# A sum over scan states: from identity matmuls to accumulated transpositions, with the mixer's end placed one or two units later

## The reference

```
h = layernorm(x) * (1 + ca) + sa;  x = x + ga * causal_attention(h)        # 8 heads, latent keys and values
h = layernorm(x) * (1 + cb) + sb;  x = x + gb * experts(h)                 # 8 small experts, best 2
h = layernorm(x) * (1 + ca) + sa;  x = x + ga * mixer(h)                   # the state-space mixer, below
h = layernorm(x) * (1 + cb) + sb;  x = x + gb * experts(h)                 # 8 experts of 512, best 2

mixer(h):  x_in, res = split(h @ in_w + in_b)                              # 256 channels each
           xc = silu(causal_conv4(x_in));  d, Bm, Cm = split(xc @ x_proj_w + x_proj_b)
           delta = softplus(d @ dt_w + dt_b);  dA = exp(delta * A);  dBx = delta * xc * Bm
           state[n, t] = dA[n, t] * state[n, t-1] + dBx[n, t]              # 16 states n per channel
           y[t] = sum over n of state[n, t] * Cm[n, t]  + xc * D_skip
           return (y * silu(res)) @ out_w + out_b
```

## Time and profile before

| | us |
|---|---|
| median of 3 runs | 1374.36 (1373.46 to 1374.67) |
| span of the profiled execution | 1379.8 |
| PE busy in the span | 1207.2 (87%) |
| DVE busy | 1037.0 (75%) |
| ACT busy | 852.2 (62%) |
| POOL busy | 489.3 (35%) |
| mean granted clock of TensorE, share of full speed | 0.95 |

### The profile page before, as it was taken

The page is one execution under the profiler, slowest core; times in us unless marked ns, Lnnn a source line. Parts: engine busy times, 40 slices in busy tenths (PEclk is TensorE's granted clock), DMA queues, the critical chain, the costliest instruction groups (busy, mean ns, idle before and its releaser), DMA issues. The chain is left out here.

```text
span 1379.8 us, 19465 instructions
## 1 busy us (share of the span) xinstructions
PE 1207.2 (87%) x6560; PEld 760.5 (55%) x6560; DVE 1037.0 (75%) x2381; ACT 852.2 (62%) x1600; POOL 489.3 (35%) x309
## 2 busy tenths in 40 slices
PE   5974689989998889989999889989899899889698
PEld 3651145655665556555656456655656556555456
DVE  3666977599866997589866997579975998569822
ACT  2634446488646966489565866479664876469332
POOL 0103930078002950069100960049300870029300
PEclk8995579999999999999999999999999999999899
DMA  7101100030001200020001200021000300011000
GB/s 245 70 16 64 60 8 1 16 108 16 16 17 55 69 12 6 16 92 31 17 9 43 88 1 17 16 78 47 16 1 16 109 16 9 1 64 60 8 1 8
DMA packets 18514, 53.22 MB, mean 39 GB/s; under 512 B 4976, under 2 KB 5864, under 8 KB 18032
## 3 DMA queue, kind: packets, MB, share of 16 engines
q1 hardware_dynamic: 16112, 43.40, 9.8%
q0 software_dynamic: 1296, 4.20, 1.0%
q10 hardware_dynamic: 1008, 4.38, 0.8%
HBM read 45.40 MB, written 2.38 MB: 35 GB/s over the span
## 5 line engine op out<-in xcount | busy, mean ns | idle before, releaser
L1482 DVE TENSOR_TENSOR_SCAN probs_T<-bank,probs_T 128x512 f32<-128x512 f32 x256 | 303.9, 1212 | 16.1 <-ACT bank L1078 12.1
L618 PEld LDWEIGHTS bank<-w_w,hidden 128*128 128x128 f32 x2048 | 248.8, 192 | 72.9 <-issue 66.8
L602 PE MATMUL bank<-hT,w_w 128*128 128x512 f32 x512 | 262.9, 629 | 27.1 <-ACT hidden L933 26.2
L447 POOL TENSOR_TENSOR probs_T<-step_space,probs_T 128x1024 f32<-128x1024 f32 x120 | 282.2, 2358 | 5.9 <-DVE probs_T L1482 5.7
L618 PE MATMUL bank<-w_w,hidden 128*128 128x128 f32 x2048 | 251.6, 276 | 2.1 <-DVE expert_sum L1174 1.6
L933 ACT ACTIVATE hidden<-bank,w_b 128x512 f32<-128x512 f32 x256 | 169.6, 686 | 117.5 <-PE bank L602 116.9
L1006 ACT ACTIVATE probs<-bank,row_neg 128x128 f32<-128x128 f32 (+3 forms) x256 | 134.8, 528 | 151.7 <-DVE row_neg L1335 134.8
L1078 ACT ACTIVATE bank<-step_space,a_neg 128x512 f32<-128x512 f32 x256 | 167.8, 683 | 55.0 <-DVE probs_T L1482 36.7
L701 PE MATMUL bank<-k_pad,q_lat 128*128 128x512 f32 (+3 forms) x512 | 185.3, 448 | 5.8 <-DMA k_pad<-xc 5.8
L1335 DVE TENSOR_REDUCE row_neg<-bank 128x1 f32<-128x128 f32 (+3 forms) x256 | 123.5, 487 | 85.1 <-PE bank L703 82.7
L602 PEld LDWEIGHTS bank<-hT,w_w 128*128 128x128 f32 x512 | 89.0, 194 | 153.0 <-ACT hidden L933 97.0
(11 more groups left out here) (183 smaller groups left out, 1577.6 us busy)
## 6 DMA issues: line engine op xcount, KB each, us to landing
probs_T<-b_rows_dram SPq DMA_DIRECT2D x64, 512.0 KB, 3.7
w_w<-in_w_dram ACTq DMA_DIRECT2D x2, 2048.0 KB, 14.0
k_pad<-xc SPq DMA_DIRECT2D x64, 64.0 KB, 2.0
x_in<-in_x_dram POOLq DMA_DIRECT2D x8, 256.0 KB, 3.3
gate<-gate_rows_dram SPq DMA_DIRECT2D x1, 2048.0 KB, 7.0
out_dram<-x_out POOLq DMA_DIRECT2D x7, 256.0 KB, 2.8
step_space<-in_wmod_dram SPq DMA_DIRECT2D x1, 768.0 KB, 5.6
probs_T<-in_wqT_dram SPq DMA_DIRECT2D x1, 512.0 KB, 4.1
```

What stands on the lines that cost most here:

```text
L447: ins = nc.gpsimd.tensor_tensor(inject[:, n % 3, :, :], u[:], row.unsqueeze(1).to_broadcast([P, DH, T]), ALU.mult)
L602: mm(hid1_bank(n)[:], w["w1"][:, n // C1, n % C1 * P:(n % C1 + 1) * P], hT[3][:], start=True, stop=True).then_inc(hid1_mm.sem, 1)
L618: ins = mm(to[:, t * P:(t + 1) * P], hidden[:, (e * C1 + c) % (2 * C1), t * P:(t + 1) * P], w["w2"][:, e * C1 + c, :], start=(c == 0), sto ...
L1482: v.tensor_tensor_scan(state[:, n % 2, c, :], decay(DH * n + c)[:], inject[:, n % 3, c, :], 0.0, ALU.mult, ALU.add).then_inc(st_ok.sem, 1)
```

## The change

PE no longer multiplies the first half's product with the identity on the left. It takes each of the product's four 128x128 tiles as the stationary operand, with the identity as the moving one, and transposes it into bank 7, accumulating over the states (`sum_first`: four instructions for each state in place of one matmul). The bank then holds the transpose of the sum, tile by tile. At the end ACT copies the bank into SBUF (`take_sum`, new, into the space of `state_sum`), and PE transposes the four tiles back into bank 7 (`turn_sum`, new), from where `mixer_end` reads as before, waiting for `sum_T` in place of `sum_mm`.

In the attention `take_sum` stands on ACT at unit 3, after the unit's exponential, and `turn_sum` on PE at unit 5. The out projection goes from unit 6 to 7, the two parts of `mixer_end` from 3 and 7 to 5 and 8, `finish` from 5 to 4, the copy of x and the layernorm from 8 to 9, and each step of the experts' head one unit later: PE's to 17, 19, 26 and 29, ACT's to 18, 23 and 27, DVE's to 21, 24 and 33. In the tail `take_sum` and `turn_sum` follow the last sum directly.

```diff
--- before.py
+++ after.py
@@ -190,6 +190,7 @@
         split = sb("split", [3 * BC, T], BF16)
         dt_in, delta, u = (step_space[:, k, :, :] for k in range(3))
         state_sum, y_skip, z = dt_in, delta, u
+        sum_rows = state_sum[:, 0, :]
 
 
         bank = [ctx.enter_context(nc.psum_tensor(f"bank{i}", [P, T], F32)) for i in range(8)]
@@ -307,6 +308,8 @@
         rd_ok = signal("rd_ok", NS)
         acc_ok = signal("acc_ok", NS - 1)
         sum_mm = signal("sum_mm", NS)
+        sum_out = signal("sum_out", 1)
+        sum_T = signal("sum_T", 1)
         z_ok = signal("z_ok", DH)
         mix_mm = signal("mix_mm", 1)
         mix_add = signal("mix_add", 1)
@@ -660,13 +663,22 @@
 
             def sum_first(n):
 
-                mm(bank[SUM_BANK][:], ident[:], read[:, n % 2, 0, :], start=(n == 0), stop=(n == NS - 1)
-                   ).then_inc(sum_mm.sem, 1)
+                for t in range(NT):
+                    ins = mm(bank[SUM_BANK][:, t * P:(t + 1) * P], read[:, n % 2, 0, t * P:(t + 1) * P], ident[:],
+                             start=(n == 0 and t == 0), stop=(n == NS - 1), is_transpose=True, skip_group_check=True)
+                ins.then_inc(sum_mm.sem, 1)
 
             def last_sum(b):
 
                 pe.wait_ge(rd_ok.sem, rd_ok.at(b, NS))
                 sum_first(NS - 1)
+
+            def turn_sum(b):
+
+                pe.wait_ge(sum_out.sem, sum_out.at(b, 1))
+                for t in range(NT):
+                    ins = tr(bank[SUM_BANK][:, t * P:(t + 1) * P], sum_rows[:, t * P:(t + 1) * P], ident[:])
+                ins.then_inc(sum_T.sem, 1)
 
             def mixer_out_mm(b):
                 pe.wait_ge(z_ok.sem, z_ok.at(b, DH))
@@ -754,6 +766,8 @@
                         scores(n)
                     if n >= LAG:
                         transposes(n - LAG)
+                    if behind and n == TURN_SUM:
+                        turn_sum(b - 1)
                     if behind and n == PE_MIXER:
                         mixer_out_mm(b - 1)
                     if not behind and n in SETUP_PE:
@@ -890,6 +904,7 @@
             main(B - 1, True, False, True)
             scan(B - 1, True)
             last_sum(B - 1)
+            turn_sum(B - 1)
             pe.wait_ge(out1_add.sem, out1_add.at(B - 2, E * NT + 1))
             mixer_out_mm(B - 1)
 
@@ -943,6 +958,10 @@
                 act.wait_ge(gap_in.sem, gap_in.at(b, layer + 1))
                 f(gap_tanh[:], gap[:], ACT.Tanh, scale=0.5).then_inc(gap_out.sem, 1)
 
+            def take_sum(b):
+                act.wait_ge(sum_mm.sem, sum_mm.at(b, NS))
+                f(sum_rows[:], bank[SUM_BANK][:], ACT.Copy).then_inc(sum_out.sem, 1)
+
             def take_queries(b, g):
                 act.wait_ge(q_mm.sem, q_mm.at(b, g + 1))
                 f(q_lat[:, g, :], bank[PRE_BANK][:], ACT.Copy).then_inc(q_out.sem, 1)
@@ -1005,6 +1024,8 @@
                         act.wait_ge(p_T.sem, p_T.at(b, n - 3))
                     f(probs_ring[:, n % 4, 0:(i + 1) * P], bank[SCORE_BANK[n % 4]][:, 0:(i + 1) * P], ACT.Exp,
                       bias=row_neg[:, n % 4:n % 4 + 1], accum_out=row_sum[:, g, i, j:j + 1]).then_inc(s_exp.sem, 1)
+                    if behind and n == LAST_SUM:
+                        take_sum(b - 1)
                     if behind and n in ACT_HEAD:
                         expert_head(b - 1, ACT_HEAD.index(n))
                     if not behind and n == SETUP_ACT:
@@ -1100,6 +1121,7 @@
             for b in range(1, B - 1):
                 iteration(b, True, True)
             iteration(B - 1, True, False)
+            take_sum(B - 1)
             expert_head(B - 1, 0)
             for n in range(E * C1):
                 if n in (2, 4):
@@ -1293,7 +1315,7 @@
                 if k == 0:
                     for c in range(DH):
                         if c == 0:
-                            dve.wait_ge(sum_mm.sem, sum_mm.at(b, NS))
+                            dve.wait_ge(sum_T.sem, sum_T.at(b, 1))
                             total = bank[SUM_BANK][:]
                         else:
                             dve.wait_ge(acc_ok.sem, acc_ok.at(b, NS - 1))
@@ -1530,9 +1552,9 @@
 PRE_UNIT = 22
 ALL_BY_ACT = 12
 LAG = 3
-LAST_SUM, LAST_READ, PE_MIXER, DVE_MIXER, FINISH, TAKE_X, NORM_UNIT = 3, 2, 6, (3, 7), 5, 8, 8
-
-PE_HEAD, ACT_HEAD, DVE_HEAD = (16, 18, 25, 28), (17, 22, 26), (20, 23, 32)
+LAST_SUM, LAST_READ, TURN_SUM, PE_MIXER, DVE_MIXER, FINISH, TAKE_X, NORM_UNIT = 3, 2, 5, 7, (5, 8), 4, 9, 9
+
+PE_HEAD, ACT_HEAD, DVE_HEAD = (17, 19, 26, 29), (18, 23, 27), (21, 24, 33)
 
 SCAN_HIDDEN = {0: (14, 17), 1: (17, 18), 2: (18, 19), 3: (19, 20), 4: (20, 22), 5: (22, 23), 6: (23, 24),
                7: (24, 26), 8: (26, 27), 9: (27, 28), 10: (28, 31), 12: (31, 32)}
```

## The result

| | before | after |
|---|---|---|
| median, us | 1374.17 (1373.46 to 1374.67) | 1446.26 (1445.42 to 1447.28) |
| ratio, 95% interval | | 1.0517 (1.0499 to 1.0536) |
| span of the profiled execution, us | 1379.8 | 1443.6 |
| mean granted clock of PE | 0.950 | 0.933 |

The changed kernel is 72 us slower. The forecast was 1423.0, or +48.6, with a range up to 1442: the sign is right, the size is too small, and the result lies 4 us outside the range. (The median of before has one more run in it than the table ahead of the prediction.)

What follows compares the result with a forecast made beforehand. DVE was taken to bound the scan, PE the attention and main stage. Six attentions at 6.4 us (38.4), the last at 4.35, tail 0.8 and clock 5 gave +48.6: median 1423.0 us, range 1391 to 1442.

Steps and rivals of the forecast that it cites:

- What bounds the kernel: DVE bounds the scan, PE the attention and main stage; idle PE costs nothing in the scan, delays the end elsewhere.
- A: Attention, scan's end to unit 8: sum's copy and turning make z and the out projection later; +0.7 us.
- B: Attention, units 14 to 19: later norm step and ACT's order make the router start later; +1.95 us.
- C: Attention, units 20 to 26: expert choice behind unit 21's maximum, PE waits at unit 22 and the gates; +1.93 us.
- D: End of the attention: the bias copy stands last on DVE, behind the next norm, and PE waits; +1.82 us.
- The scan: Scan stage: PE saves 0.40 us per state, but the stage is DVE's, so nothing is gained.
- The rival that named the clock in the scan: Scans: transpositions leave PE too little active, half speed there, about 1600 us; chance 0.03.
- The tail: After the last sum: transpositions, ACT's copy, turning and hand-overs stand where 1.12 us stood; +0.8 us.
- The clock: Attention's end: D's idle PE brings half speed for 3.4 us, 1.7 us each in three of six batches; +5 us.
- a rival at 0.10: Attentions: the clock falls in every batch, at two places; 43.5 + 24, so 1442 us; chance 0.10.

Runs made afterwards that it cites:

- e5: Changed kernel with extra, unused multiplications on PE inside four waits of an attention, all waits kept: 1438.29 us, ratio 1.0437.
- e6: Kernel before with extra multiplications in the wait at a scan's start and in the first scan's last four states: 1370.22 us, ratio 0.9953.
- e1: Changed kernel with the transposed sum kept, but x, its norm and the experts' head back at their old units: 1393.52 us, ratio 1.0110.
- e7: Changed kernel with x and the norm's steps, transposition and scaling back at their old units, the rest late: 1434.08 us, ratio 1.0401.
- e4: Changed kernel with the router's copy on ACT and the expert choice on DVE back at units 22 and 20: 1422.30 us, ratio 1.0317.
- e3: Changed kernel with DVE's last head step, the copy of the experts' bias sum, back at unit 32: 1425.87 us, ratio 1.0341.
- e11: Kernel before with only DVE's copy of the experts' bias sum moved from unit 32 to 33: 1397.59 us, ratio 1.0133.
- e8: e1 with the product of C issued three times instead of once in every state of a scan: 1391.68 us, ratio 1.0100.
- e9: e1 with four transpositions of a constant added in every state of a scan, ahead of C's product: 1390.23 us, ratio 1.0089.

## Why the prediction was wrong

**What bounds the kernel: right.** That idle time of PE costs nothing by itself in the scan and everything in the attention held. With the clock held up in the attentions (e5), +46.8 us stand against 38.4 + 4.35 = 42.75 predicted for A to D. PE's clock in the scan does cost something (e6, and below).

**A: mechanism right, +0.7 predicted, 1.4 measured (e1).** The copy of the sum on ACT was put 4.08 us behind the start of the attention and came at 4.12; DVE's mixer end was put at 5.38 and came at 5.47; the out projection was to wait 1.6 us and waits 1.63. The turning waits 0.44, not 0.7. What was missed is the 0.50 at unit 14, which stays in e1 and e7 and so belongs to the mixer's late end and not to the norm.

**B: right, +1.95 predicted, 1.74 (e7).** The router's wait is 1.31 against 1.3; at unit 14 half of the 0.93 is A's, as said.

**C: right in size, +1.93 predicted, 2.22 (e4), the last step misplaced.** DVE starts to choose right behind unit 21's maximum and takes the 2.7 us that were read off. But PE waits once, 2.59 us at unit 22's transpositions, and not 1.4 there and 1.3 at the gates: it waits for the copy at 722.40, which empties their bank and stands on DVE behind two more maxima, the next norm's first step and a normalising. When PE comes to the gates after that (725.23) they are there.

**D: right, +1.82 predicted, 1.74 (e3), 1.75 in e11.** The last copy stands behind the norm's 1.11 us as foreseen, and PE waits 1.97 us, where about 2 was said.

**The scan: zero predicted, +3.5 us.** The saving of PE work in it was read right (four transpositions hand over after 0.43 to 0.49 us where the old sum took 0.87), and it is worth nothing to DVE's stage, as predicted. That it can cost something was not seen: with less work per state PE's clock falls in the middle of the scan (e1 against e8 and e9). The rival that named the clock in the scan had it at 0.50 throughout, which it is not.

**The tail: +0.8 predicted, 1.4.**

**The clock: this is the step that failed.** It was sized at three falls, +5 us; 14 falls in the attentions cost 19 us (after against e5), and those in the scans the 3.5 us more. The step took D's wait as the only one that a fall can follow, and let it have one in half of the batches. For D by itself that was near: e11 has four falls in seven attentions, at 1.6 us where 1.7 was said. No row stood behind the half, so that is in part luck. But A, B and C leave waits of the same size, 1.3 to 2.6 us, and those were counted as idle time and left out of the count of falls, though the earlier trace rows show a fall behind a wait of that kind. Of the 14 falls five stand at D's wait, nine at B's and C's, none at A's. The upper end of the term, two falls in each of seven attentions, +24, came in number, at 1.4 us each; it stood as a rival at 0.10, with 1442, and the range ended at that rival's value.

The sum with the measured terms: 46.8 of waits, 19.3 and 3.5 of clock, 1.4 in the tail, together 71 of the 72 us.

## What to carry to other kernels

A wait on an engine whose clock can fall behind it has two prices: its length, and, some of the time, a stretch at half speed behind it (here 1.4 to 1.6 us). When a change adds waits to the engine that bounds a stage, list all of them for the clock, not only the longest, and let the range take the case in which each brings a fall. Work taken from an engine that has time to spare is not always free of cost either: here it was the filling between two waits.

## What the hardware showed that was not expected

- The same wait is followed by a fall at one moment and not at another: 1.97 us of it cost 1.75 us in three attentions and 3.3 to 3.4 in three others (e11). A change can move falls into a stage that it does not touch: e5 and e7 have 7 to 8 us more in the scans than after, for edits in the attention.
- Adding useless products made kernels faster: 20 to 26 in an attention took 1.3 to 4.4 us off it (e5), 9 at a scan's start about 1 us off each scan that had a fall (e6).
- Transpositions added to each state held the granted clock up as products did (e9), and accumulating ones cost what single ones cost: four of them into the bank of the sum hand over to the next instruction after 0.49 us (688.95 to 689.44 in the trace after), where the product with the identity took 0.87.
